# A tile of key weights moved to another place in SBUF, and two setup steps reordered, in a two-layer graph kernel

## The reference

```python
# layer 0
h = jnp.maximum(_layernorm(x), 0.0)
x = x + einsum('bnm,bmo->bno', adj, einsum('bni,io->bno', h, weight)) + bias
# layer 1, per graph, 8 heads, dim 256
h = jnp.maximum(_layernorm(x), 0.0)
feat_proj = (h @ fc_w + fc_b).reshape(bs, n, 8, 256).transpose(0, 2, 1, 3)
q = feat_proj @ q_w + q_b
k = feat_proj @ k_w + k_b
logits = q + swapaxes(k, -1, -2)
masked = leaky_relu(logits + (1.0 - adj) * -1e9, 0.01)
attn = softmax(masked, axis=-1)
out = (attn @ feat_proj) ... @ fp_w + fp_b + h
x = x + sigmoid(out)
```

## Time and profile before

| | |
|---|---|
| median of 3 runs | 1406.87 us (1406.33 to 1406.88) |
| the profiled execution, its own time | 1406.65 us |
| its span, first to last instruction | 1404.9 us |
| granted TensorE clock | 1.000 of 2.4 GHz |
| PE, DVE, ACT, POOL busy | 1394.7, 1285.1, 1126.5, 1102.0 us |

### The profile page before, as it was taken

One profiled execution on the slowest core, in us unless ns is written; L12 is line 12 of the kernel. 1 busy time (PEld: TensorE's weight loads), 2 busy tenths in 40 slices (PEclk: granted clock), 3 DMA queues, 4 the chain that ended last, 5 costly groups with the idle time before them and its releaser, 6 DMA issues.

```text
span 1404.9 us, 31603 instructions
## 1 busy us (share of the span) xinstructions
PE 1394.7 (99%) x9048; PEld 1252.5 (89%) x9048; DVE 1285.1 (91%) x4408; ACT 1126.5 (80%) x3429; POOL 1102.0 (78%) x1295
## 2 busy tenths in 40 slices
PE   9999999999999999999999999999999999999998
PEld 7898899899899889998998898998989989988987
DVE  7999999999999999999999999999999999998996
ACT  4878788788888888887888888888878878887876
POOL 4788878878778878778787788787787887888764
PEclk9999999999999999999999999999999999999999
DMA  7423323323223233233232232232332322322221
GB/s 238 98 63 107 107 54 106 91 69 106 71 88 106 55 105 106 54 105 97 63 106 80 79 106 61 99 106 54 105 103 58 106 88 73 106 67 85 77 61 41
DMA packets 177132, 124.69 MB, mean 89 GB/s; under 512 B 137808, under 2 KB 143568, under 8 KB 177104
## 3 DMA queue, kind: packets, MB, share of 16 engines
q1 hardware_dynamic: 176816, 124.35, 30.3%
q10 hardware_dynamic: 288, 0.01, 0.0%
HBM read 105.98 MB, written 18.35 MB: 89 GB/s over the span
## 4 chain that ended last, share of the span: by engine, by line
PE 94%; POOL 2%; issue 1%; DVE 1%; DMA 1%; ACT 0%; POOLq 0%; SPq 0%; ACTq 0%; DVEq 0%
PE gbank L381 48%; PE ybank L381 24%; PE tbank L481 8%; PE bank L381 6%; PE bank L426 4%; PE bank L462 2%; PE bank L449 2%; DMA late<-key_rows 0%; POOL att L1561 0%; POOL att L1554 0%; DMA qk<-qk_w_dram 0%; DVE att L829 0%; POOL xb L1544 0%; POOL t_pos L1546 0%; POOL ends L1577 0%
## 5 line engine op out<-in xcount | busy, mean ns | idle before, releaser
L1233 ACT ACTIVATE att<-att 128x128 f32<-128x128 f32 x1024 | 397.8, 393 | 47.0 <-DVE att L836 44.0
L381 PE MATMUL gbank<-m_hi,hT_lo 128*128 128x512 f32 x1024 | 426.7, 417 | 0.0
L1554 POOL TENSOR_TENSOR att<-late,t_pos 128x512 f32<-128x512 f32 x256 | 330.6, 1293 | 120.5 <-PE tbank L481 115.8
L381 PE MATMUL gbank<-m_hi,hT_hi 128*128 128x512 f32 x1024 | 403.2, 394 | 0.0
L381 PE MATMUL gbank<-m_lo,hT_hi 128*128 128x512 f32 x1024 | 401.3, 392 | 0.0
L812 DVE TENSOR_TENSOR g_lo<-gbank,g_hi 128x512 fp32r<-128x512 f32 x512 | 341.4, 678 | 47.1 <-ACT g_hi L1226 42.0
L1561 POOL TENSOR_TENSOR att<-att,rinv 128x512 f32<-128x512 f32 x256 | 289.4, 1131 | 107.1 <-DVE rinv L841 106.5
L1226 ACT ACTIVATE g_hi<-gbank 128x512 fp32r<-128x512 f32 x512 | 291.1, 595 | 39.6 <-PE gbank L381 39.4
L829 DVE TENSOR_SCALAR_CACHE_REDUCE att<-att,qs 128x128 f32<-128x128 f32 x1024 | 291.6, 341 | 27.0 <-POOL att L1554 26.7
L381 PE MATMUL ybank<-g_hi,pT_hi 128*128 128x256 f32 x1016 | 281.5, 277 | 0.0
L381 PE MATMUL ybank<-g_hi,pT_lo 128*128 128x256 f32 x1016 | 281.4, 277 | 0.0
(11 more groups left out here) (97 smaller groups left out, 2323.1 us busy)
## 6 DMA issues: line engine op xcount, KB each, us to landing
late<-key_rows SPq DMA_DIRECT2D x64, 1024.0 KB, 6.1
g_in<-graph_dram SPq DMA_DIRECT2D x64, 512.0 KB, 3.4
out_dram<-ends SPq DMA_DIRECT2D x63, 256.0 KB, 3.9
qs<-key_rows SPq DMA_DIRECT2D x128, 4.0 KB, 2.5
key_rows<-kq_sb SPq DMA_DIRECT2D x64, 24.0 KB, 1.4
att<-fc_wT_dram SPq DMA_DIRECT2D x4, 256.0 KB, 5.6
late<-fp_w_dram SPq DMA_DIRECT2D x4, 256.0 KB, 5.3
ends<-fp_w_dram SPq DMA_DIRECT2D x2, 512.0 KB, 7.9
```

The costliest lines, as they stand in the source:

```text
L381: mm = pe.matmul(out_ap, w, m, start=first and n == 0, stop=last and n == len(terms) - 1)
L1233: e = act.activation(a[:, s], a[:, s], ACT.Exp, scale=-1.0, bias=a[:, CH + h:CH + h + 1], accum_out=esum[j][c][:, h:h + 1])
L1554: gp.tensor_tensor(a, keys[q][:, j, c * HC:(c + 1) * HC, :], t_pos[q][:, j, :].unsqueeze(1).broadcast_to([P, HC, P]), ALU.add)\
```

## The change

The program gets an unused tile `line` of 384 bytes ahead of `u`, and `u` itself grows: each of its two halves now begins 512 bytes after the other, of which the first 256 are used. By this `u` stands at 192 modulo 512 with both halves, and all tiles behind it move by 896 bytes, that is by -128 modulo 512 and by nothing modulo 128: `ident` to 192, `g_in`, `h0_f`, `h1` to 160, the blocks of `att` to 224, 240, 256 and 272. The tiles ahead of `u` stay.

```diff
-        u = sb("u", [P, DT, 2 * HALF], F32R, LINE)
+        sb("line", [P, 6 * LINE // 4], F32, LINE)
+        u_all = sb("u", [P, DT, P], F32R, LINE)
+        u = u_all[:, :, 0:2 * HALF]
...
                 warm()
-                key_query_bias()
                 fold(0)
                 fold(1)
                 fold(2)
+                key_query_bias()
                 aggregate(0, 0)
...
                 stats0(0, 0)
+                mean0(0, 0)
                 bias_rows()
-                mean0(0, 0)
                 bias_part(0)
...
-                act.activation(u[:], none[:], ACT.Copy).then_inc(a_none, 1)
+                act.activation(u, none[:], ACT.Copy).then_inc(a_none, 1)
```

## The result

The changed kernel takes 1420.36 us (median of 4 runs, 1420.17 to 1421.11), before took 1406.88 beside it. The ratio is 1.0099, with an interval of 1.0086 to 1.0112: 13.5 us slower, where 1.0 us faster was forecast. The profiled execution has a span of 1419.2 us, 14.3 over that of before.

A forecast was written before the change was run, and what follows sets the result against it. PE, busy 99% of the span, was taken as the bound. The terms -0.8 (`queries_keys`), +0.3 (`ident`), 0 (other hand-overs) and -0.5 (setup) sum to -1.0 us, for a median of 1405.9 us, range 1403.8 to 1407.3.

The forecast's parts named there:

- The failed step: PE's 256-column products in the loop: a 64-byte distance between weights and moving operand was said to go with 113 ns each.
- the part on what bounds the kernel: Whole kernel: PE is busy 99% of the span, so only its product pace and the start of the stream count.
- The `queries_keys` term: Loop, `queries_keys` products: `u` at 192 saves 4.2 ns in three streams per pair, -0.8 us, bounds 0 to -1.6.
- the excess: `queries_keys` products in the loop: 117.5 ns each against 113.3 for other 256-column products, 4.2 ns laid to the place of `u`.
- What moves along: Loop hand-overs with moved `ident`, `att`, `h1`, `h0_f`: +0.3 us for `ident`, 0 for five others with bounds +-1.3.
- The setup: Start of the kernel: earlier `mean0` and later bias product let PE reach 46.58 us sooner, -0.5 us, bounds 0 and -0.9.
- the latest that was forecast: Setup: the first `aggregate` on PE was to start at 9.5 to 9.7 us instead of 10.20.
- the one on the slow side: Loop: `ident` leaves +64 ahead of 320 loads of `hT_lo`, costing 1.3 to 2.6 us; 1408.2 at 8 ns; chance 0.13.
- The sign that was named for a wrong prediction: Loop: distance between neighbouring repetitions changing by more than 30 ns per pair, or a new PE wait behind 50 us.

The follow-up runs named there:

- the five kernels above that lie between: Follow-up kernels that make only part of the change's moves against the kernel before; the text does not list which five.
- distance 128: Kernel before with `w0`, `m`, `g` placed 128 bytes ahead of the weights loaded beside them, modulo 512, instead of 64; its total time is not given.
- behind `ident`: Kernel before with 384 unused bytes after `ident`, so only the tiles after it move by -128 modulo 512; 1411.30 us, ratio 1.0033.
- distances 128 and 448: Two kernels: before with `w0`, `m`, `g` 128 or 448 bytes ahead of the weights loaded beside them, modulo 512, instead of 64; the latter 1426.44 us.
- distances 0 and 256: Two kernels: before with `w0`, `m`, `g` 0 or 256 bytes ahead of the weights loaded beside them, modulo 512, instead of 64; 1427.28 and 1427.41 us.
- distance 192: Kernel before with `w0`, `m`, `g` 192 bytes ahead of the weights loaded beside them, modulo 512, instead of 64; 1426.53 us.
- distance 0: Kernel before with `w0`, `m`, `g` at the same place modulo 512 as the weights loaded beside them, instead of 64 ahead; 1427.28 us.

## Why the prediction was wrong, by its steps

**The failed step** is in the part on what bounds the kernel: "their weights stand 64 bytes ahead of the moving operand modulo 512" (the places given beside it, 256 against 320, mean 64 bytes lower) was taken as the reason for 113 ns. It is not sufficient. With the same distance, the same products run at 113.3 or at 117.8 ns. In which of the two they run is handed on from the products ahead of them, through the 512-column products in between. Those also show it: their distances go 225.8, 229.2, 231.7 in turn, three alike in sum for either case. In the loop a short run came where the last of them ahead of the run was 231.7, in before, after and the five kernels above that lie between. A long one came where it was 225.8 or 229.2, or another value.

**The `queries_keys` term**, -0.8 us: it moved by 469 - 467 = 2 ns per pair, 0.1 us, in the changed kernel, and by the same 2 ns with `u` unmoved and the rest moved. So moving `u` did not take away the excess that the prediction laid to its place. It changed only how the time is spread: the first of the four products takes 114.1 ns in the changed kernel and the fourth 118.4, before 117.5 and 117.5. The rule of the Trainium skill that the prediction quotes ("TensorE: Matmul & The Clock Gate", the section on how a matmul runs, LDWEIGHTS step) would have given 0 for this term, near what was measured. It does not carry over to the kernel as a whole. `u` is only ever loaded and never streamed, and moving it alone cost 4.4 us. So where a loaded tile stands can change the time of the streams. Moving only the streaming tiles by 64 bytes made 1427.28 us out of 1406.9. By what the load acts on the stream is not shown.

**What moves along**, +0.3 with bounds of -1.3 and +2.6 us: measured at the moved steps themselves, it is as small as said: transposes and `aggregate` are together 6 ns per pair shorter. The missing term is the one that none of the steps has: the effect of a hand-over on the 60 products of other steps that follow it, 0.25 us per pair, 64 times. The prediction weighed each hand-over by its own 4.2 ns.

**The setup**, -0.5 us with bounds of 0 and -0.9: its mechanism was right in the steps where the trace of the setup alone can tell, though the first `aggregate` came 0.36 us later than the latest that was forecast. It measures -0.8 us at the last wait of the filling. In the time it is -1.0 between the medians, with 1 inside the interval of the ratio. It can't be told from what differs between executions either: with the order of before, the same transposes start anywhere from 45.5 us (only `u` moved) to 47.1 us (distance 128). What was not foreseen is PE's idle time of 1.96 us ahead of fold 0 in the changed kernel's profiled execution, behind which the clock fell. Against the 0.98 us of before, 0.13 us is that of the bias product which no longer stands there, 0.65 us comes from the warm-up products that ended earlier, and 0.20 us from folds that began later. In the profile of the setup alone the idle time was 1.09 us and the clock did not fall. Nor are slow folds a mark of the new order: with the order of before, the twelve records of folds 0 to 2 took 4.27 to 4.91 us in five profiles (the rest moved, `ident`, behind `ident`, distances 128 and 448), against 2.96 in before's.

**The rivals**: the one on the slow side named `ident` and its hand-overs, of which `ident` is right. It priced them at 4 to 8 ns each and so gave 1408.2. The sign that was named for a wrong prediction, more than 30 ns per pair between repetitions, is what the trace shows: 250.

What stays open is what the state is. That it is some order in time between the weight load's and the stream's reads is a reading of the facts that it depends on addresses, on what ran ahead and on an idle PE. A rival is that another engine's accesses slow PE, since the steps of DVE, ACT and POOL keep in time with PE's. Against it stands that the distance is the same in all twelve places of a run while such steps begin and end beside it: in before's run at 603.58 us DVE is idle from 604.13 to 604.82, POOL begins steps at 603.65, 603.80 and 603.95 and ACT one at 604.67, and the distance stays at 113.3 ns. No run tested it by itself. No run looked at the reads themselves, and no rule came out of these by which the outcome of a new layout could be told.

## What to carry to other kernels

When a kernel stands at PE's pace, a change of layout can move the pace of products whose tiles it does not touch. Compare the distances between starts of like products over the whole loop, place by place, and not only at the tiles that were moved. A place in SBUF that was found good by trial holds for one sequence of instructions on PE, and one more instruction in the loop can undo it. So pad such a change out to keep all other tiles where they were modulo 512, and then read the run behind the changed step as well. Here the padding took the layout's loss from 14.0 to 4.4 us, and the run behind `queries_keys` was the one that stayed long.

## What the runs showed of the hardware that had not been expected

- The same product of 256 columns with a 128-column weight load beside it has two steady paces, 113.3 and 117.8 ns, at the granted clock of 2.4 GHz. Either persists through dozens of products of two shapes, through some hand-overs and for over a thousand microseconds of repetitions. After the one wait in before's loop one run was at 117.8 ns, and the next at 113.3 again.
- Places of the streaming tiles that differ by 256 bytes give the same pace and time: distances 0 and 256 give 1427.28 and 1427.41 us, 192 and 448 give 1426.53 and 1426.44, against 1406.9 at 64. Whether the distance to the loading tile counts or the place alone is open.
- One more transpose of 0.109 us per pair, with no address changed, made the kernel 13.0 us slower, of which its own time is 7.0.
- A `transform` at distance 192 begins with 121.7 ns and comes down to 113.3 within four products; at distance 0 one begins with 113.3 and goes up to 120.0 within three. So a pace can be an end state, and not only a property of the pair.
- PE sat idle for 1.96 us near the start of the changed kernel, and 0.5 us into the work behind it the granted clock fell to 1.2 GHz for 3.4 us. Twelve records took 4.57 us there, and 1.98 + 1.14 with 2.4 GHz in the kernel with the setup alone.
